# Last stage of an attention and feed-forward kernel: VectorE's gated product placed ahead of Newton's steps, ScalarE's gate and square ahead of the normalisations

## The chip, the cores and the metric

The kernel runs on one core of a Trainium2 chip. The metric is the device time of one execution in microseconds (us). The engines are TensorE (PE in the profile; its weight loads are PEld), VectorE (DVE), ScalarE (ACT), GpSimd (POOL) and SyncE (SP), which here issues all the transfers. Each engine runs its own list of instructions in order and waits on semaphores for the others.

## The reference

A pre-norm transformer layer in fp32: attention, then a gated channel mix that also looks at the token before. The change touches only the second half.

```python
x = x + attention(layernorm(x))               # x: 4 x 2048 x 256, 16 heads of 16
h = layernorm(x)
h_prev = h shifted by one token (zero at the start of a sequence)
hr = mu_r * h + (1 - mu_r) * h_prev
hk = mu_k * h + (1 - mu_k) * h_prev
r = sigmoid(hr @ W_r.T)
k = square(relu(hk @ W_k.T))
x = x + r * (k @ W_v.T)
```

## The kernel before

The 8192 tokens are cut into 16 blocks of 512. A first stage makes q, k and v, a second does attention for 64 steps, and the last stage (`stage_mix`) does the output projection, the second layer norm and the channel mix, block by block, software-pipelined in pairs of blocks (b, b+1 with b even). Nothing schedules at build time: the order on each engine is the order in which its Python function issues calls, and `Steps` objects are semaphores that count named steps ("gated" of block 3, say). The names of the steps:

- `proj(b)` (TensorE, L447) multiplies the attention heads by the output weights; `residual(b)` (VectorE, L367) adds x to it, which gives x1, and takes statistics (L371).
- `means(pair)` (VectorE, L378 to L386) combines the statistics of a pair of blocks and makes a seed for the reciprocal root. `newton(pair)` (L394, L396, L398 three times, then L402) refines it: ten operations on 128x8 elements, all of whose inputs lie in SBUF, and each waits for the one before. The last one gives the offset. Pair p is blocks 2p and 2p+1.
- `normalise(b)` (ScalarE, L1670, four operations) waits for the offset; `turned(b)` (TensorE, L457) transposes its four results one by one; `keep_turned(b)` (ScalarE, L1682 and L1688) copies them out of PSUM and scales them by mu.
- `shift(b)` (VectorE, L412 or L410, then L417 twice for mk and twice for mr) adds the shares of the token before.
- `key(b)` (TensorE, L1783) needs the mk part of `shift(b)`, `receptance(b)` (L1795, weights r) the mr part. `keep_gate(b)` (ScalarE, L1706) is the sigmoid of the receptance, `square(b)` (ScalarE, L1696 relu and L1700 square) works on the key, `value(b)` (TensorE, L1795, weights v) multiplies the square.
- `gated(b)` (VectorE, L1735) multiplies value(b) from PSUM by the gate. `finish(b)` (GpSimd, L1646) adds x1, and SyncE stores the block.
- GpSimd also does `heads(b)` (L321, two operations: attention sums times inverse denominators, for `proj(b)`) and `add_to_x(b)` (L330: x plus bias, for `residual(b)`), in this order for an even b: finish(b), heads(b+6), finish(b+1), add_to_x(b+6), heads(b+7), add_to_x(b+7). Both wait for transfers of their inputs.

TensorE's order in a pair is key(b), receptance(b), value(b), receptance(b+1), key(b+1), turned(b+2), proj(b+4), value(b+1), turned(b+3), proj(b+5). key(b) writes the two PSUM banks that value(b-1) was in, so it waits for gated(b-1):

```python
        elif blk < LAST - 1:
            vy.wait(te, blk - 1, "gated")
```

In the last pairs there is no projection left: after key(13) come turned(14), turned(15), value(13), key(14). value(b) waits for square(b). In this section and below a "pair b" is the stretch from key(b) to key(b+2) on TensorE.

Of the kernel before, what the change touches and what calls it, by code (L numbers as in the profile page):

```python
# [22 lines left out]
B, N, C, H = 4, 2048, 256, 16  # L23
# [4 lines left out]
BLOCKS = B * N // TB  # L28
# [173 lines left out]
class MixInputs:  # L202
# [156 lines left out]
    def residual(self, dve, blk, banks):  # L359

        s = blk % 2
        self.gx.wait(dve, blk, "xb")
        if blk >= SUMS:
            self.gy.wait(dve, blk - SUMS, "y")
        for b in range(2):
            self.pf.wait(dve, blk, ("proj0", "proj")[b])
            self.dx.done(dve.tensor_tensor(self.rows_of(self.x1[blk % SUMS][:, 2 * b:2 * b + 2, :]), banks[b],  # L367
                                      self.rows_of(self.x_sb[s][:, 2 * b:2 * b + 2, :]), ALU.add))
        for t in range(TT):
            self.dx.wait(dve, blk, f"x1{t // 2}")  # L370
            self.ln.done(dve.bn_stats(self.stats[:, s * TT + t, :], self.x1[blk % SUMS][:, t, :]))  # L371
# [1188 lines left out]
def stage_mix(ctx, nc, psum, inputs, out):  # L1560
# [22 lines left out]
    EARLY, LAST = inputs.EARLY, BLOCKS - 1  # L1583

    def turned_at(blk):

        return OUT if blk == LAST else TURNED

    def key_at(blk):
        return {LAST - 1: TURNED, LAST: OUT}.get(blk, KEY)  # L1590

    def rec_at(blk):
        return {0: TURNED, LAST: KEY}.get(blk, REC)

    def squares_of(blk):

        if blk < LAST:
            return inputs.kr, inputs.ka
        return [x1[n % SUMS].rearrange("p t c -> p (t c)").rearrange("p (k t) -> p k t", k=KH)
                for n in (LAST - 5, LAST - 4)]  # L1600

    def after(eng, sem, value):
        if value > 0:
            eng.wait_ge(sem, value)

    def rows_of(t):
        return t.rearrange("p t c -> p (t c)")

    def banks(n):
        return psum[:, n:n + 2, :].rearrange("p a c -> p (a c)")  # L1610
# [52 lines left out]
    def scalar(ac):  # L1663
        def normalise(blk):
            ln.wait(ac, blk // 2, "offset")
            if blk >= 2:
                pt.wait(ac, blk - 2, "turned1")
            for t in range(TT):
                at_t = blk % 2 * TT + t
                an.done(ac.activation(xn[blk % 2][:, t, :], x1[blk % SUMS][:, t, :], ACT.Identity,  # L1670
                                      bias=work[:, 5, at_t:at_t + 1], scale=work[:, 2, at_t:at_t + 1]))

        def keep_turned(blk):

            s = blk % 2
            for k in range(KH):
                pt.wait(ac, blk, f"turned{k}")
                if blk >= 1:
                    vb.wait(ac, blk - 1, "prev")
                if blk >= 2:  # L1680
                    vb.wait(ac, blk - 2, f"mr{KH - 1}")
                at.done(ac.copy(xT[s][:, k, 1:TB + 1], psum[:, turned_at(blk) + k, :]))  # L1682
            for n in ("mk", "mr"):
                if blk >= 2:
                    (pk if n == "mk" else pr).wait(ac, blk - 2, n[1])
                for k in range(KH):
                    at.wait(ac, blk, f"xT{k}")
                    at.done(ac.activation(mixed[n][s][:, k, :], xT[s][:, k, 1:TB + 1], ACT.Copy,  # L1688
                                          scale=col[n][:, k:k + 1]))

        def square(blk):
            kr, ka = squares_of(blk)
            pk.wait(ac, blk, "k")
            if blk == LAST:
                gy.wait(ac, LAST - 4, "y")
            ab.done(ac.activation(kr[:, :, :], psum[:, key_at(blk):key_at(blk) + 2, :], ACT.Relu))  # L1696
            ab.wait(ac, blk, "relu")
            if 1 <= blk < LAST:
                pv.wait(ac, blk - 1, "v")
            ab.done(ac.activation(ka[:, :, :], kr[:, :, :], ACT.Square))  # L1700

        def keep_gate(blk):
            pr.wait(ac, blk, "r")
            if blk >= 2:
                vy.wait(ac, blk - 2, "gated")
            ag.done(ac.activation(rows_of(gate[blk % 2]), banks(rec_at(blk)), ACT.Sigmoid))  # L1706

        for steps in (ab, ag):
            steps.start(ac)
        for blk in range(0, BLOCKS, 2):  # L1710
            more = blk + 2 < BLOCKS
            square(blk)
            keep_gate(blk)
            if more:
                normalise(blk + 2)
                keep_gate(blk + 1)
                normalise(blk + 3)
                square(blk + 1)
            else:
                square(blk + 1)  # L1720
                keep_gate(blk + 1)
            if more:
                for n in range(2):
                    keep_turned(blk + 2 + n)

    def vector(dve):
        def residual(blk):
            inputs.residual(dve, blk, [psum[:, OUT + b, :] for b in range(2)])

        def gated(blk):  # L1730
            s = blk % 2
            pv.wait(dve, blk, "v")
            ag.wait(dve, blk, "gate")
            after(dve, s_out[s], DMA * (blk // 2))
            vy.done(dve.tensor_tensor(rows_of(y[s]), banks(key_at(blk)), rows_of(gate[s]), ALU.mult))  # L1735

        def last_half(half):

            s, at_t = LAST % 2, slice(2 * half, 2 * half + 2)
            pv.wait(dve, LAST, ("half", "v")[half])  # L1740
            if half == 0:
                ag.wait(dve, LAST, "gate")
                dve.wait_ge(s_out[s], DMA * (LAST // 2))
            vy.done(dve.tensor_tensor(rows_of(y[s][:, at_t, :]), psum[:, key_at(LAST) + half, :],
                                      rows_of(gate[s][:, at_t, :]), ALU.mult))
            vy.wait(dve, LAST + half, "gated")
            dve.tensor_tensor(y[s][:, at_t, :], y[s][:, at_t, :], x1[LAST % SUMS][:, at_t, :], ALU.add
                              ).then_inc(s_last, 1)

        vy.start(dve)  # L1750
        for blk in range(0, BLOCKS, 2):
            gated(blk)
            if blk == 0:
                for n in range(inputs.SLICES):
                    inputs.invert(dve, B - 1, n)
            if blk + 4 < BLOCKS:
                residual(blk + 4)
            if blk + 2 < BLOCKS:
                inputs.shift(dve, blk + 2)
            if blk + 1 < LAST:  # L1760
                gated(blk + 1)
            else:
                for half in range(2):
                    last_half(half)
            if blk + 4 < BLOCKS:
                residual(blk + 5)
            if blk + 2 < BLOCKS:
                inputs.shift(dve, blk + 3)
            if blk + 4 < BLOCKS:
                inputs.means(dve, blk // 2 + 2)  # L1770
                inputs.newton(dve, blk // 2 + 2)

    def key(te, blk):
        vb.wait(te, blk, f"mk{KH - 1}")
        if blk == 0:
            dx.wait(te, 2 * EARLY - 1, "x11")
        elif blk < LAST - 1:
            vy.wait(te, blk - 1, "gated")
        else:
            at.wait(te, blk, "xT1")  # L1780
        for h in range(KH):
            for k in range(KH):
                mm = te.matmul(psum[:, key_at(blk) + h, :], w_sb["k"][:, k, h * P:(h + 1) * P],  # L1783
                               mixed["mk"][blk % 2][:, k, :], start=(k == 0), stop=(k == KH - 1))
        pk.done(mm)
# [6 lines left out]
    def tensor(te):  # L1792
# [41 lines left out]
        for blk in range(0, BLOCKS, 2):  # L1834
# [16 lines left out]
            if more:  # L1851
                turned(blk + 3)
                proj(blk + 5)

    return sync, gpsimd, scalar, vector, tensor, first_key


def build(nc, a):
# [7 lines left out]
    with ExitStack() as ctx:  # L1866
# [4 lines left out]
        first = stage_attend(ctx, nc, psum, a["x"], a["wqT"], a["wkT"], a["wvT"], a["bq"], a["bk"], q_d, k_d, kd_d, v_d,  # L1871
                             sums_d, attend_inputs, mix_inputs)
        last = stage_mix(ctx, nc, psum, mix_inputs, a["out"])
        block = ctx.enter_context(nc.Block())

# [47 lines left out]
```

## Time and profile before

| | us |
|---|---|
| median of three runs | 2774.69 (2774.01 to 2775.11) |
| the profiled execution | 2775.01 |
| its span in the trace | 2773.2 |
| last stage in that span, from key(0) on | 2541.7 to the end, 231.5 |
| TensorE busy in 2600 to 2650 | 48.42 of 50.00 |
| VectorE, ScalarE, GpSimd busy there | 37.72, 26.09, 27.14 |
| granted TensorE clock in the last stage | 1.00 (2.4 GHz) |

The span is what the trace covers; the device time of the same execution is 1.8 us longer. Times in the trace count from the start of the span. A row of the timeline is a run of equal instructions, so its length is from the start of the first to the end of the last, and "idle before" is how long its engine had nothing to do, with what ended that.

### The profile page before, as it was taken

How to read it: one execution, taken by the hardware profiler on the slowest of the kernel's cores; microseconds unless marked ns; L12 is line 12 of the kernel's file. 1: busy time of each engine (PE TensorE's matmuls, PEld its weight loads, DVE VectorE, ACT ScalarE, POOL GpSimd, SP SyncE). 2: the span in 40 equal slices, each digit the busy share in tenths (PEclk: the TensorE clock that was granted, in tenths of full speed). 3: DMA queues.
4: the chain of work that ended last, by engine and by line, in shares of the span. 5: the costliest groups of instructions: out<-in, count | busy, mean ns of one | idle time of the engine just before them, and what ended most of it. 6: DMA issues, size and time to landing. Idle time of an engine off the chain costs nothing.

```text
span 2773.2 us, 60078 instructions
## 1 busy us (share of the span) xinstructions
PE 2737.5 (99%) x23666; PEld 927.5 (33%) x23666; DVE 2496.9 (90%) x4853; ACT 2489.6 (90%) x2863; POOL 372.7 (13%) x751
## 2 busy tenths in 40 slices
PE   9999999999999999999999999999999999999999
PEld 6552222222222222222222222222222222224776
DVE  5658999999999999999999999999999999975774
ACT  7768999999999999999999999999999999997555
POOL 6761000000000000000000000000000000103551
PEclk9999999999999999999999999999999999999999
DMA  6642010000000000000010101010101100212531
GB/s 196 208 150 66 12 30 14 22 20 20 22 22 22 22 22 22 23 20 25 11 30 9 33 11 33 12 33 11 33 12 38 29 19 22 59 40 83 163 127 46
DMA packets 135290, 124.36 MB, mean 45 GB/s; under 512 B 49888, under 2 KB 117344, under 8 KB 135008
## 3 DMA queue, kind: packets, MB, share of 16 engines
q1 hardware_dynamic: 135008, 120.52, 14.1%
q8 instruction: 187, 3.06, 0.5%
q14 instruction: 95, 0.78, 0.1%
HBM read 72.75 MB, written 47.19 MB: 43 GB/s over the span
## 4 chain that ended last, share of the span: by engine, by line
PE 81%; SPq 10%; ACT 4%; DVE 2%; DMA 2%; issue 2%; POOL 0%; ACTq 0%; POOLq 0%
PE psum L1364 33%; PE psum L1267 17%; PE psum L1323 15%; PE psum L1392 4%; SPq L153 3%; PE psum L1795 3%; SPq L158 2%; PE psum L1282 2%; PE psum L1405 2%; SPq L126 2%; PE psum L447 2%; SPq L127 2%; DMA a_qs<-q_parts 2%; PE psum L1783 2%; ACT m_gate L963 1%
## 5 line engine op out<-in xcount | busy, mean ns | idle before, releaser
L1045 DVE TENSOR_REDUCE a_mx<-psum 128x1 f32<-128x512 f32 x3096 | 1946.5, 683 | 108.9 <-PE psum L1323 88.4
L1267 PE MATMUL psum<-a_qs,a_ks 50*128 50x512 f16 x4096 | 791.7, 383 | 10.2 <-ACT p_x L963 0.5
L963 ACT ACTIVATE m_gate<-psum 128x1024 f32<-128x1024 f32 x684 | 674.7, 1034 | 37.1 <-PE psum L1267 34.4
L963 ACT ACTIVATE m_y<-psum 128x1024 f32<-128x1024 f32 x682 | 672.7, 1034 | 37.7 <-PE psum L1267 34.8
L1323 PE MATMUL psum<-a_ks,a_qs 48*128 48x512 f16 x3596 | 695.0, 383 | 11.5 <-DVE a_mx L1045 2.4
L963 ACT ACTIVATE p_x<-psum 128x1024 f32<-128x1024 f32 x682 | 672.7, 1034 | 37.3 <-PE psum L1267 34.6
L1364 PE MATMUL psum<-m_gate,a_vst 128*32 128x256 f32 (+1 forms) x4568 | 413.1, 433 | 0.8
L1364 PE MATMUL psum<-p_x,a_vst 128*32 128x256 f32 (+1 forms) x4568 | 412.0, 432 | 0.8
L1364 PE MATMUL psum<-m_y,a_vst 128*32 128x256 f32 (+1 forms) x4552 | 411.8, 433 | 0.8
L1267 PEld LDWEIGHTS psum<-a_qs,a_ks 50*128 50x128 f16 x4096 | 198.8, 93 | 604.7 <-issue 139.6
L1040 DVE CUSTOM_DVE_ANT_0 a_copied<-psum,a_copied 128x512 f32<-128x512 f32 x500 | 323.4, 684 | 22.0 <-PE psum L1323 22.0
L1323 PEld LDWEIGHTS psum<-a_ks,a_qs 48*128 48x128 f16 x3596 | 174.9, 93 | 462.6 <-DVE a_mx L1045 367.2
L972 ACT ACTIVATE a_copied<-psum 128x1024 f32<-128x1024 f32 x250 | 260.5, 1042 | 0.1
L830 POOL MEMSET a_mx<- 128x8 f32 x64 | 7.2, 112 | 1380.5 <-DVE a_m L1024 1345.2
L823 POOL COPY a_vst<-a_vin 128x64 f32<-128x64 f32 x256 | 59.7, 236 | 751.5 <-PE psum L1364 751.5
L1364 PEld LDWEIGHTS psum<-m_gate,a_vst 128*32 128x32 f32 x4568 | 90.4, 107 | 189.8 <-issue 174.7
L1364 PEld LDWEIGHTS psum<-p_x,a_vst 128*32 128x32 f32 x4568 | 90.6, 107 | 189.3 <-issue 173.8
L1364 PEld LDWEIGHTS psum<-m_y,a_vst 128*32 128x32 f32 x4552 | 90.1, 107 | 189.1 <-issue 173.8
L1282 PE MATMUL psum<-a_kd,a_qs 48*128 48x512 f16 x500 | 97.2, 381 | 0.0
L845 POOL TENSOR_TENSOR m_split<-m_whole,m_split 128x512 f16<-128x512 f32 x64 | 73.5, 1159 | 58.4 <-ACT m_split L951 42.1
L949 ACT ACTIVATE m_whole<-psum,p_sb,p_gain 128x512 f32<-128x512 f32 x64 | 49.7, 777 | 34.8 <-PE psum L1392 34.8
L367 DVE TENSOR_TENSOR m_whole<-psum,m_x 128x512 f32<-128x512 f32 x24 | 16.4, 688 | 59.5 <-PE psum L447 59.5
(149 smaller groups left out, 1644.0 us busy)
## 6 DMA issues: line engine op xcount, KB each, us to landing
m_x<-x SPq DMA_DIRECT2D x24, 512.0 KB, 5.7
a_qs<-q_parts SPq DMA_DIRECT2D x384, 32.0 KB, 2.1
sums<-a_o SPq DMA_DIRECT2D x256, 34.0 KB
q_parts<-m_split SPq DMA_DIRECT2D x16, 512.0 KB, 3.2
v_rows<-m_v SPq DMA_DIRECT2D x16, 512.0 KB, 2.8
k_parts<-m_split SPq DMA_DIRECT2D x16, 512.0 KB, 3.9
a_ks<-k_parts SPq DMA_DIRECT2D x64, 128.0 KB
a_vin<-v_rows SPq DMA_DIRECT2D x64, 128.0 KB, 5.7
```

What stands on the lines that cost most here:

```text
L153: sp.dma_start(self.qs[row:row + D, it % QRING, :].rearrange("p (u t) -> p u t", u=GP), src[a, par]).then_inc(self.s_q, DMA)
L845: least.done(pool.tensor_tensor(parts[s][:, j, 1, :], full[s][:, j, :], parts[s][:, j, 0, :], ALU.subtract))
L963: ac.activation(p_sb[n % WEIGHTS][:, 2 * pair:2 * pair + 2, :], psum[:, at:at + 2, :], ACT.Exp, scale=SCALE).then_inc(s_exp, 1)
L972: ac.activation(copied[:, :, :], psum[:, at:at + 2, :], ACT.Relu).then_inc(s_exp, 1)
L1040: dve.tensor_tensor_reduce(out=copied[:, par, :], in0=psum[:, bank(at), :], in1=copied[:, par, :], scale=1.0, scalar=LEAST, op0=ALU.add, o ...
L1045: dve.tensor_reduce(peak, psum[:, bank(at), :], AX.X, ALU.max).then_inc(s_mx, 1)
L1267: mm = te.matmul(psum[:, pair_of_banks(u) + par, :], ks[row:row + MR, (it // QB) % 2, pair, c * P:(c + 1) * P], qs[row:row + MR, it % QRIN ...
L1282: mm = te.matmul(psum[:, pair_of_banks(u) + par, :], qs[row:row + SR, pit % QRING, at:at + P], kd[row:row + SR, (pit // QB) % 2, pair, :], ...
L1323: te.matmul(psum[:, bank(slot(n, par)), :], qs[row:row + SR, pit % QRING, at:at + P], keys, start=True, stop=True).then_inc(s_sp, 1)
L1364: mm = te.matmul(psum[32 * g:32 * g + 32, O, at:at + width], v_st[:, c, g, :], p_sb[n % WEIGHTS][:, g, at:at + width], start=(c == 0), sto ...
L1392: mm = te.matmul(psum[:, j % 2, :], w_sb[n][:, k, h * P:(h + 1) * P], xnT[blk % 2][:, k, :], start=(k == 0), stop=(k == KH - 1))
L1795: mm = te.matmul(psum[:, bank + t // 2, (t % 2) * C:(t % 2 + 1) * C], lhsT[:, k, t * P:(t + 1) * P], w[:, k, :], start=(k == 0), stop=(k = ...
```

## The change

Three moves, all in `stage_mix`. No instruction is added or removed, except that the listing below groups neighbours.

1. VectorE: gated(b), for even b from 2 to 14, now stands in front of newton, directly after means (for b = 14, where there is no newton, its place is as before). Before, it came after newton, as the first call of the next round.
2. VectorE, first pair only: gated(1) now stands between residual(4) and shift(2), before after shift(2).
3. ScalarE: before, the order was normalise(b+2), keep_gate(b+1), normalise(b+3), square(b+1), keep_turned(b+2), keep_turned(b+3); now it is keep_gate(b+1), normalise(b+2), square(b+1), normalise(b+3), and then the same.

```diff
@@ scalar
             square(blk)
             keep_gate(blk)
             if more:
+                keep_gate(blk + 1)
                 normalise(blk + 2)
-                keep_gate(blk + 1)
+                square(blk + 1)
                 normalise(blk + 3)
-                square(blk + 1)
+                for n in range(2):
+                    keep_turned(blk + 2 + n)
@@ vector
-        for blk in range(0, BLOCKS, 2):
-            gated(blk)
-            if blk == 0:
-                for n in range(inputs.SLICES):
-                    inputs.invert(dve, B - 1, n)
-            if blk + 4 < BLOCKS:
-                residual(blk + 4)
-            if blk + 2 < BLOCKS:
+        gated(0)
+        for n in range(inputs.SLICES):
+            inputs.invert(dve, B - 1, n)
+        residual(4)
+        gated(1)
+        inputs.shift(dve, 2)
+        for blk in range(0, LAST - 1, 2):
+            if blk:
+                if blk + 4 < BLOCKS:
+                    residual(blk + 4)
                 inputs.shift(dve, blk + 2)
-            if blk + 1 < LAST:
                 gated(blk + 1)
...
             if blk + 4 < BLOCKS:
                 residual(blk + 5)
-            if blk + 2 < BLOCKS:
-                inputs.shift(dve, blk + 3)
+            inputs.shift(dve, blk + 3)
             if blk + 4 < BLOCKS:
                 inputs.means(dve, blk // 2 + 2)
+            gated(blk + 2)
+            if blk + 4 < BLOCKS:
                 inputs.newton(dve, blk // 2 + 2)
+        for half in range(2):
+            last_half(half)
```

The orders of TensorE, GpSimd and SyncE are the same in both. On VectorE, in the first pair, with the gated product as L1735 before and L1734 after:

```order
-L1735 TENSOR_TENSOR m_y<-psum,m_gate 128x1024
+L1734 TENSOR_TENSOR m_y<-psum,m_gate 128x1024
 L291 RECIPROCAL m_inv<-m_den 128x32 x8
 L367 TENSOR_TENSOR m_x<-psum,m_x 128x512 x2
 L371 BN_STATS m_stats<-m_x 128x6 x4
+L1734 TENSOR_TENSOR m_y<-psum,m_gate 128x1024
 L412 COPY m_xT<-m_xT 128x2
 L417 SCALAR_TENSOR_TENSOR m_split<-m_xT,m_restmk,m_split 128x512 x2
 L417 SCALAR_TENSOR_TENSOR m_split<-m_xT,m_restmr,m_split 128x512 x2
-L1735 TENSOR_TENSOR m_y<-psum,m_gate 128x1024
```

gated(1) moved past the five instructions of shift(2). On VectorE, in a later pair, between the seed (L386) and Newton's first step (L394):

```order
 L382 TENSOR_SCALAR m_work<-m_work 128x8
 L386 TENSOR_SCALAR m_work<-m_work 128x8
+L1734 TENSOR_TENSOR m_y<-psum,m_gate 128x1024
 L394 TENSOR_TENSOR m_work<-m_work 128x8
 L396 SCALAR_TENSOR_TENSOR m_work<-m_work 128x8
```

The even block's product now stands there; it is gone from its place behind the last of the ten steps (L402). On ScalarE, in the same pair, after the even block's square (L1696, L1700):

```order
-L1706 ACTIVATE m_gate<-psum 128x1024
-L1670 ACTIVATE m_xn<-m_x,m_work 128x256 x4
-L1706 ACTIVATE m_gate<-psum 128x1024
+L1706 ACTIVATE m_gate<-psum 128x1024 x2
 L1670 ACTIVATE m_xn<-m_x,m_work 128x256 x4
 L1696 ACTIVATE m_v<-psum 128x1024
 L1700 ACTIVATE m_v<-m_v 128x1024
+L1670 ACTIVATE m_xn<-m_x,m_work 128x256 x4
 L1682 COPY m_xT<-psum 128x512 x2
```

The two gates stand together, then come the first normalisation, the square, and the second normalisation.

## Rows read from the trace of the kernel before

**Rows 1.** Timeline of PE, pair 4: start us, us, engine line op out<-in xcount [idle]

```profile
2602.34 3.60 PE L1783 MATMUL psum<-m_split,m_wk 128*128 128x512 f32 x8
...
2612.74 3.72 PE L1795 MATMUL psum<-m_wr,m_split 128*128 128x256 f32 x16
2617.18 3.67 PE L1783 MATMUL psum<-m_split,m_wk 128*128 128x512 f32 x8 [0.71 <-DVE m_y L1735]
2620.68 1.04 PE L457 MATMUL psum<-m_ident,m_xn 128*128 128x128 f32 x8
...
2632.80 3.60 PE L1783 MATMUL psum<-m_split,m_wk 128*128 128x512 f32 x8
```

**Rows 2.** Timeline of DVE, same pair: means, Newton's steps, gated(4).

```profile
2605.87 3.40 DVE L417 SCALAR_TENSOR_TENSOR m_split<-m_xT,m_restmk,m_split 128x512 f32<-128x512 f32 x2
...
2612.61 0.63 DVE L378 BATCH_NORM_AGGREGATE m_mv<-m_stats 128x2 f32<-128x6 f32 x8
...
2613.89 0.17 DVE L394 TENSOR_TENSOR m_work<-m_work 128x8 f32<-128x8 f32 x1
...
2615.70 0.17 DVE L402 SCALAR_TENSOR_TENSOR m_work<-m_mv,m_work 128x8 f32<-128x8 f32 x1
2615.80 1.22 DVE L1735 TENSOR_TENSOR m_y<-psum,m_gate 128x1024 f32<-128x1024 f32 x1
```

**Rows 3.** Timeline of ACT, same pair: normalise(6).

```profile
2615.90 2.07 ACT L1670 ACTIVATE m_xn<-m_whole,m_work 128x256 f32<-128x256 f32 x4 [5.44 <-DVE m_work L402]
```

**Rows 4.** Timeline of POOL, same pair: finish(4).

```profile
2617.11 2.36 POOL L1646 TENSOR_TENSOR m_y<-m_y,m_x 128x1024 f32<-128x1024 f32 x1 [4.97 <-DVE m_y L1735]
```

**Rows 5.** Timeline of all engines: a Newton step beside a GpSimd addition.

```profile
2543.57 2.35 POOL L330 TENSOR_TENSOR m_x<-m_x,m_bo 128x1024 f32<-128x1024 f32 x1 [1.97 <-DMA m_x<-x]
2543.61 2.33 DVE L394 TENSOR_TENSOR m_work<-m_work 128x8 f32<-128x8 f32 x1
```

**Rows 6.** Timeline of PE, first pairs: value(1) and key(2).

```profile
2564.55 3.62 PE L1795 MATMUL psum<-m_wv,m_v 128*128 128x256 f32 x16
...
2572.93 3.67 PE L1783 MATMUL psum<-m_split,m_wk 128*128 128x512 f32 x8 [0.43 <-DVE m_y L1735]
```

**Rows 7.** Timeline of DVE, first pairs: shift(2), gated(1), residual(5), shift(3).

```profile
2567.95 2.38 DVE L417 SCALAR_TENSOR_TENSOR m_split<-m_xT,m_restmk,m_split 128x512 f32<-128x512 f32 x2
...
2571.57 1.21 DVE L1735 TENSOR_TENSOR m_y<-psum,m_gate 128x1024 f32<-128x1024 f32 x1
2572.71 1.27 DVE L367 TENSOR_TENSOR m_x<-psum,m_x 128x512 f32<-128x512 f32 x2
...
2575.22 0.14 DVE L412 COPY m_xT<-m_xT 128x2 f32<-128x2 f32 x1
```

**Rows 8.** Timeline of POOL, first pairs: heads(6), add_to_x(6), add_to_x(7).

```profile
2566.62 2.49 POOL L321 TENSOR_TENSOR m_hT<-m_num,m_rden 128x512 f32<-128x512 f32 x2 [9.43 <-DMA m_rden<-inverse_denominators]
...
2577.54 2.81 POOL L330 TENSOR_TENSOR m_x<-m_x,m_bo 128x1024 f32<-128x1024 f32 x1 [2.31 <-DMA m_x<-x]
...
2587.76 2.36 POOL L330 TENSOR_TENSOR m_x<-m_x,m_bo 128x1024 f32<-128x1024 f32 x1 [4.96 <-DMA m_x<-x]
```

**Rows 9.** Timeline of PE, pair 12: value(12), receptance(13), value(13).

```profile
2731.55 3.62 PE L1795 MATMUL psum<-m_wv,m_v 128*128 128x256 f32 x16
2735.00 3.62 PE L1795 MATMUL psum<-m_wr,m_split 128*128 128x256 f32 x16
...
2744.26 3.72 PE L1795 MATMUL psum<-m_wv,m_v 128*128 128x256 f32 x16 [0.46 <-ACT m_v L1700]
```

**Rows 10.** Timeline of DVE, same pair: gated(12).

```profile
2735.20 1.23 DVE L1735 TENSOR_TENSOR m_y<-psum,m_gate 128x1024 f32<-128x1024 f32 x1 [2.32 <-PE psum L1795]
```

**Rows 11.** Timeline of ACT, same pair: normalise(15), square(13), keep_turned(14).

```profile
2739.57 2.06 ACT L1670 ACTIVATE m_xn<-m_whole,m_work 128x256 f32<-128x256 f32 x4
2742.09 1.03 ACT L1696 ACTIVATE m_v<-psum 128x1024 f32<-128x1024 f32 x1 [0.45 <-PE psum L1783]
...
2744.11 1.06 ACT L1682 COPY m_xT<-psum 128x512 f32<-128x512 f32 x2
```

More of the change, by code:

```diff
@@ L1721, in scalar @@
                 keep_gate(blk + 1)
-            if more:
-                for n in range(2):
-                    keep_turned(blk + 2 + n)
     def vector(dve):
@@ L1750, in vector @@
         vy.start(dve)
-        for blk in range(0, BLOCKS, 2):
-            gated(blk)
-            if blk == 0:
-                for n in range(inputs.SLICES):
-                    inputs.invert(dve, B - 1, n)
-            if blk + 4 < BLOCKS:
-                residual(blk + 4)
-            if blk + 2 < BLOCKS:
+        gated(0)
[8 more added lines that the diff above has]
+                    residual(blk + 4)
                 inputs.shift(dve, blk + 2)
-            if blk + 1 < LAST:
                 gated(blk + 1)
-            else:
-                for half in range(2):
-                    last_half(half)
             if blk + 4 < BLOCKS:
                 residual(blk + 5)
-            if blk + 2 < BLOCKS:
-                inputs.shift(dve, blk + 3)
+            inputs.shift(dve, blk + 3)
             if blk + 4 < BLOCKS:
                 inputs.means(dve, blk // 2 + 2)
+            gated(blk + 2)
+            if blk + 4 < BLOCKS:
                 inputs.newton(dve, blk // 2 + 2)
+        for half in range(2):
+            last_half(half)
     def key(te, blk):
```

## The prediction

> **What bounds the kernel now.** I read the timeline of TensorE first, then those of the engines that it waits for. In the last stage TensorE works nearly without a gap, so a gain can only come out of its gaps. The one that repeats: receptance(5) starts at 2612.74, key(5) at 2617.18 [rows 1]. A stage of sixteen such matmuls takes 3.45 from start to start (2731.55 to 2735.00) [rows 9], 3.5 behind a wait (2617.18 to 2620.68) [rows 1]; key(5) could have started at 2616.25 and is 0.93 late, with VectorE's gated product named as releaser. The reason stands in the order of VectorE [rows 2]: means begin at 2612.61, Newton's steps at 2613.89, the product only at 2615.80. Four pairs (4, 6, 8, 10) look like this. key(2) has a gap of 0.43 for gated(1) [rows 6], and value(13) one of 0.46 for square(13) [rows 9]. The prize is thus about 4 x 1.0 + 0.5 + 0.5, 5 us of 2775: 0.18% at the very best. (A measurement of this kernel can tell about 0.2%, 5.5 us, from no change.)
>
> **What comes in place of the gap, pairs 4 to 10.** gated(4) moves ahead by Newton's ten steps. Means to product takes 1.18 (the product follows its predecessor by 0.10, L394 stands 1.28 behind L378) [rows 2], so it starts at G = 2613.79 and ends at 2615.01. key(5) goes at 2616.25: the gap is gone, with 1.2 us to spare, and turned(6) could start at 3.44 more, 2619.69 (no wait ahead of it).
> But GpSimd's finish(4) starts 1.31 after the product does (2615.80 to 2617.11) and runs 2.36 [rows 2, 4]. Before, VectorE had nothing to do then. Now Newton's steps begin at G + 1.14 (2571.57 to 2572.71 for what follows a product) [rows 7], and the second at G + 1.34, 0.03 after finish(4). What a small VectorE step does beside a GpSimd addition can be seen once [rows 5]: L394, 0.17 us long elsewhere [rows 2], took 2.33, from 0.04 after the addition began until it ended. So the second step waits until G + 1.31 + 2.36 = G + 3.67; eight more follow at 0.20 each (1.81 for nine from 2613.89 to 2615.70) [rows 2], the last starts at G + 5.12 and normalise(6) 0.20 later [rows 2, 3], at G + 5.3 = 2619.1. Its 2.07 us end at 2621.2; the last two transposes need some 0.3 behind that (0.05 from releaser to start, two of eight transposes in 0.88, the rate of a restart). proj(8) starts at 2621.5. Before, it started at 2620.68 + 0.88 = 2621.56 [rows 1]. The 0.93 is given back almost exactly one stage later: **-0.1 per pair, -0.35 for four** (between -0.6, if the step wins the port from GpSimd now and then, and 0). Everything behind proj keeps its distance to it: square(5) follows normalise(6) and is done 1.5 before value(5), and shift(6) waits for proj(8) anyway. Covered by this: the later normalise(7) and keep_turned(6), some 2 us nearer to their users, 1 us or more left.
> The rows show this for L394 and not for a small SCALAR_TENSOR_TENSOR (seven of the ten steps). The Trainium skill ("SBUF — State Buffer", section "Who interferes with whom") says that a VectorE instruction with two SBUF inputs contends with a GpSimd one that reads SBUF, and that the later one blocks until the first is done. All ten steps have two such inputs; the rule speaks against this change, and L394 at 2.33 agrees. Without such a rule the sum would be the lock-free rival below.
>
> **First pair and pair 2.** gated(1) can start 3.65 after value(1) does (2731.55 to 2735.20 for block 12) [rows 9, 10]: 2564.55 + 3.65 = 2568.20 [rows 6]. finish(1), which was at 2572.86, now goes at 2569.50 to 2571.86, and shift(2) begins at 2569.34, right under it. A blocked mk pair ends 1.22 after GpSimd lets go (heads(6) until 2569.11, pair until 2570.33) [rows 7, 8]: 2573.08. key(2) starts at 2573.14, against 2572.93 before [rows 6]: +0.2 where -0.5 was meant.
> shift(3) suffers more. From the end of mk to the end of mr is 1.24 (2570.33 to 2571.57), and residual(5) with its statistics takes 2.51 (2572.71 to 2575.22) [rows 7], so shift(3) begins at 2573.08 + 1.24 + 2.51 = 2576.83, 1.6 later than before. add_to_x(6) comes at 2577.54, when its input lands [rows 8], heads(7) behind it; before, shift(3) was nearly through. Now GpSimd gets the port after the first mk step, at 2577.76, holds it 2.21 (its end was 2580.35, 2.21 after shift(3) let it in), and the other three steps go one by one between its operations: 0.55 after 2579.97, then 1.70 each, as beside heads(9) (3.40 for two) [rows 2]: 2583.9. receptance(3) could start at 2573.14 + 3.5 + 2 x 3.45 = 2583.55; it starts at 2583.97, **+0.4**, and key(3) at 2587.5, turned(4) at 2590.9.
> Then Newton again: means at 2583.85, G = 2585.05, the steps from 2586.2, the ninth at 2587.80 and the tenth at 2588.0. add_to_x(7) starts at 2587.76, when its input lands [rows 8]; nothing in the change moves that transfer. It blocks the ninth step until 2590.1, and finish(2), which is next on GpSimd, blocks the tenth until 2592.45. normalise(4) runs from 2592.5 to 2594.55, and proj(6) starts at 2594.85, where the free order of TensorE gives 2591.75. Before, key(2) at 2572.93 and 3.5 + 4 x 3.45 + 0.88 behind it gave 2591.1. So **pair 2 ends 3.7 later than before**. This hangs on 0.04 us for the second block and on 0.25 for the first: if the ninth step slips in ahead, normalise(4) goes at 2590.2 and the pair loses 1.4; if both do, 0.65.
>
> **Pair 12, the last.** Here value(12) sets the product: G = 2735.20 [rows 10]. The same Newton delay puts normalise(14) at G + 5.3 = 2740.5 to 2742.6, so square(13), which was at 2742.09 [rows 11], goes at 2742.5; and normalise(15), which stood ahead of it (2739.57), now stands behind it. square takes 2.02 (2742.09 to 2744.11) [rows 11], normalise 2.07: 2746.6. turned(15) is ahead of value(13) on TensorE, and needs it: value(13) starts at 2746.87 against 2744.26 [rows 9], **+2.6**. Until the end TensorE then waits for nothing else: keep_turned(14), shift(14), gated(13) are 2.4 later, less than that. In the other pairs this move costs nothing, since proj and value stand between.
>
> **Sum:** +3.7 - 0.35 + 2.6 = +6.0, a profiled execution of 2781.0, and against the median of 2774.69 (0.32 below the profiled one) **2780.7**.
>
> **Rivals.**
> (a) *One step slips in*, or both, in pair 2: +1.4 or +0.65 in place of +3.7, so 2778.4 or 2777.6: no difference to be measured. For it: the margin is a few hundredths. Against: I counted no waits but those in rows, and any more makes it two.
> (b) *Not slower, lock-free*: Newton's steps run at 0.20 beside GpSimd. Then key(2) wins 0.6 and pairs 4 to 10 win 1.0 each; pair 12 still loses 2.2 (normalise(15) behind square(13): 2744.1 + 2.07 + 0.3 = 2746.45). Sum -2.4, 2772.3. Against it: [rows 5]. It decides from the point where Newton's second step ends before G + 2.
> (c) *Faster by 0.2%* would need lock-free and no loss in pair 12: 2769.5. ScalarE's order forbids it.
> (d) *Every pair pays*: add_to_x(b+5) ended 1.65 before G in pair 4. Should its input land that much later, it blocks Newton's steps too, up to 2.36 per pair: 2783 and more. Against it: that transfer keeps its distance to proj.
>
> **How the numbers follow.** Forecast with two blocks 0.45, (a) 0.39 (0.27 and 0.12), (b) 0.05, (c) 0.03, (d) and other losses 0.08. The range reaches from (a) at 2777.6 less 0.5 for its terms to 2782.0, the forecast with 0 for -0.35 and a later transfer: 2777.0 to 2782.0. The bound of 0.2% is 2780.24, half a microsecond under the forecast, so a quarter of its chance counts as no change: slower 0.41 (0.34 + 0.07), same 0.55, faster 0.04.
>
> **What would show it.** Right: key(5), key(7), key(9), key(11) without a wait, but turned(6) and so on waiting for normalise; one step of Newton of some 2.3 us directly behind each even product; two of them in pair 2; receptance(3) late; value(13) near +2.6 over its place. Wrong: Newton's steps all at 0.17, or proj(8) more than 0.3 nearer to key(4) than 19.2 us (2602.34 to 2621.56) [rows 1], or a ScalarE wait in pair 12 that is not for VectorE's offset.

## The result, and the profile after

| | us |
|---|---|
| before, median of 16 | 2774.15 |
| after, median of 16 | 2778.64 (2777.42 to 2785.48) |
| ratio | 1.0018, 95% interval 1.0011 to 1.0025 |
| the profiled execution of after | 2783.50, its span 2781.7 |

The change makes the kernel 4.5 us slower, inside the range of 2777.0 to 2782.0 and 2.1 below the 2780.7 that was forecast. (0.5 of these 2.1 come from the base: the forecast stood on a median of three, 2774.69, and that of sixteen is 2774.15. As a change it was +4.5 for a forecast of +6.0.) Of the 16 executions nine lie between 2777.4 and 2778.8, four between 2779.3 and 2780.1, and three (one of them the profiled one) above 2782: they are not all alike, and the reading of one trace alone would mislead. So two more executions of the same program were profiled (after_look1 and after_look2, below).

The measure used from here on is the length of a pair, from key(b) to key(b+2) on TensorE. It leaves out the stages ahead of key(0), which is at 2541.3 to 2544.5 in the fourteen profiles of this case, whatever the kernel.

| pair | before | forecast | after | look1 | look2 |
|---|---|---|---|---|---|
| 0 | 31.23 | 31.44 | 31.43 | 31.45 | 31.44 |
| 2 | 29.41 | 32.9 | **34.03** | **34.63** | 29.45 |
| 4 | 30.46 | 30.37 | 29.78 | 29.79 | 29.90 |
| 6 | 30.70 | 30.6 | 30.73 | 30.71 | 30.69 |
| 8 | 30.45 | 30.36 | 30.40 | 30.38 | 30.43 |
| 10 | 30.71 | 30.6 | 30.67 | 30.69 | 30.70 |
| 12 | 23.16 | 25.8 | 27.26 | 25.69 | 27.12 |
| key(14) to last value | 17.22 | 17.22 | 17.22 | 17.22 | 17.23 |

Timeline of TensorE in the profile of after, pair 6, the answer to [rows 1] (start us, us, engine line operation, idle before and its releaser). key(7) is the second row:

```profile
2647.99 3.72 PE L1795 MATMUL psum<-m_wr,m_split 128*128 128x256 f32 x16 [0.22 <-DVE m_split L417]
2651.54 3.60 PE L1783 MATMUL psum<-m_split,m_wk 128*128 128x512 f32 x8
2655.09 1.82 PE L457 MATMUL psum<-m_ident,m_xn 128*128 128x128 f32 x8
2656.75 3.62 PE L447 MATMUL psum<-m_wo,m_hT 128*128 128x256 f32 x16
```

key(7) has no wait any more (the 0.22 ahead of receptance(7) is the wait for shift(7), 0.15 before). The eight transposes of turned(8), which took 1.04 in [rows 1], take 1.82, since they wait one by one for ScalarE. VectorE in the same stretch, the answer to [rows 2]:

```profile
2649.04 1.22 DVE L1734 TENSOR_TENSOR m_y<-psum,m_gate 128x1024 f32<-128x1024 f32 x1
2650.18 0.16 DVE L394 TENSOR_TENSOR m_work<-m_work 128x8 f32<-128x8 f32 x1
2650.37 2.34 DVE L396 SCALAR_TENSOR_TENSOR m_work<-m_work 128x8 f32<-128x8 f32 x1
```

and GpSimd and ScalarE, the answers to [rows 4] and [rows 3]:

```profile
2650.34 2.35 POOL L1646 TENSOR_TENSOR m_y<-m_y,m_whole 128x1024 f32<-128x1024 f32 x1 [3.62 <-DVE m_y L1734]
```
```profile
2654.35 2.08 ACT L1670 ACTIVATE m_xn<-m_whole,m_work 128x256 f32<-128x256 f32 x4 [1.58 <-DVE m_work L402]
```

The product starts at G = 2649.04, finish(6) at G + 1.30, the second of Newton's steps at G + 1.33, and it waits to the end of that addition: an instruction on 128x8 elements takes 2.34. normalise(8) starts at G + 5.31, as the forecast had it to 0.01.

Pair 2 of the same profile: VectorE's steps of Newton that are not 0.15 to 0.17 long, and GpSimd beside them, the answer to [rows 8]:

```profile
2587.45 2.26 DVE L398 SCALAR_TENSOR_TENSOR m_work<-m_work 128x8 f32<-128x8 f32 x1
2589.75 2.26 DVE L394 TENSOR_TENSOR m_work<-m_work 128x8 f32<-128x8 f32 x1
```
```profile
2587.35 2.34 POOL L330 TENSOR_TENSOR m_x<-m_x,m_bo 128x1024 f32<-128x1024 f32 x1 [3.68 <-DMA m_x<-x]
2589.65 2.34 POOL L1646 TENSOR_TENSOR m_y<-m_y,m_whole 128x1024 f32<-128x1024 f32 x1
```

Two steps are held, the sixth behind add_to_x(7), the seventh behind finish(2). Pair 2 and pair 12 on TensorE, the latter to be read beside [rows 9]:

```profile
2593.39 2.08 PE L457 MATMUL psum<-m_ident,m_xn 128*128 128x128 f32 x8 [1.97 <-ACT m_xn L1670]
2595.26 4.60 PE L447 MATMUL psum<-m_wo,m_hT 128*128 128x256 f32 x16
...
2749.62 2.08 PE L457 MATMUL psum<-m_ident,m_xn 128*128 128x128 f32 x8 [2.14 <-ACT m_xn L1670]
2751.49 4.99 PE L1795 MATMUL psum<-m_wv,m_v 128*128 128x256 f32 x16
2756.32 3.60 PE L1783 MATMUL psum<-m_split,m_wk 128*128 128x512 f32 x8
```

Both places have something that the forecast did not: behind a wait of about 2 us, sixteen matmuls of 128x256 take 4.60 and 4.99 where they take 3.62 elsewhere. The granted clock (the figure of 1.00, 0.60 and so on, behind the busy times of PE, PEld, DVE, ACT and POOL) shows why:

```profile
2588.00:2593.30 5.30, 3.42 (x8) 1.15 (x7) 4.47 (x5) 1.68 (x3) 3.99 (x2) 1.00 0.44 159
2593.30:2596.00 2.70, 2.61 (x10) 1.92 (x11) 0.00 (x0) 2.67 (x5) 0.00 (x0) 0.60 0.47 155
2596.00:2600.00 4.00, 4.00 (x17) 3.40 (x17) 0.80 (x2) 4.00 (x8) 0.00 (x0) 0.85 0.00 0
2600.00:2604.00 4.00, 4.00 (x24) 3.57 (x23) 3.95 (x9) 2.10 (x4) 2.51 (x2) 1.00 0.46 134
...
2749.50:2752.00 2.50, 2.27 (x10) 1.51 (x11) 0.06 (x1) 2.50 (x6) 0.00 (x0) 0.77 0.02 7
2752.00:2756.00 4.00, 4.00 (x15) 3.34 (x14) 2.84 (x5) 4.00 (x8) 0.00 (x0) 0.72 0.01 2
```

TensorE was at 2.4 GHz (1.00) until it had idled for 1.97 us, then fell to 1.2 GHz for part of the next two windows (0.60 and 0.85), and was back at 2600. From the start of proj(6) to that of value(3) are 4.44 us in place of 3.45: the clock cost 1.0 there, and 1.3 in pair 12 (value(13) to key(14) is 4.83 against 3.56 before; with the slower transposes of turned(15) it is 1.6, the difference between pair 12 here and in look1).

The wait in pair 12 comes from ScalarE, to be read beside [rows 11]. normalise(15) stood ahead of square(13) there; now it is the row of 2748.89, behind it, and turned(15) waits for it:

```profile
2744.92 2.08 ACT L1670 ACTIVATE m_xn<-m_whole,m_work 128x256 f32<-128x256 f32 x4 [0.84 <-DVE m_work L402]
2746.90 1.00 ACT L1696 ACTIVATE m_v<-psum 128x1024 f32<-128x1024 f32 x1
...
2748.89 2.06 ACT L1670 ACTIVATE m_xn<-m_whole,m_work 128x256 f32<-128x256 f32 x4
```

### The profile page after: what moved, and what is told of

The parts are those of the page before. It is cut to its first block, busy times and chain, and to the rows that moved or that the text cites. A ratio compares the mean times of both kernels' runs of the same rounds, so it can differ in the third digit from the quotient of the medians.

```text
span 2781.7 us, 60078 instructions
## 1 busy us (share of the span) xinstructions
PE 2744.8 (99%) x23666; PEld 928.7 (33%) x23666; DVE 2511.6 (90%) x4853; ACT 2489.4 (89%) x2863; POOL 374.8 (13%) x751
## 4 chain that ended last, share of the span: by engine, by line
PE 80%; SPq 9%; ACT 4%; DVE 3%; issue 2%; DMA 2%; POOL 0%; ACTq 0%; POOLq 0%
PE psum L1364 33%; PE psum L1267 17%; PE psum L1323 15%; PE psum L1392 4%; SPq L153 3%; PE psum L1282 2%; SPq L158 2%; PE psum L1405 2%; PE psum L1795 2%; PE psum L447 2%; SPq L126 2%; SPq L127 2%; DMA a_qs<-q_parts 2%; ACT m_gate L963 1%; ACT p_x L963 1%
## 5 line engine op out<-in xcount | busy, mean ns | idle before, releaser
L963 ACT ACTIVATE m_gate<-psum 128x1024 f32<-128x1024 f32 x684 | 674.3, 1033 | 37.2 <-PE psum L1267 34.4
L1706 ACT ACTIVATE m_gate<-psum 128x1024 f32<-128x1024 f32 x16 | 16.4, 1024 | 56.6 <-PE psum L1795 56.6
```

The costliest lines, as they stand in the source:

```text
L963: ac.activation(p_sb[n % WEIGHTS][:, 2 * pair:2 * pair + 2, :], psum[:, at:at + 2, :], ACT.Exp, scale=SCALE).then_inc(s_exp, 1)
```

## The experiments

The theory after this reading had four parts. (1) In pairs 4 to 12 finish(b), which the product itself releases, holds one of Newton's steps, and that costs what key(b+1) gains. (2) In pair 2 it depends on when the input of add_to_x(7) lands. (3) In pair 12 there is no stage left that covers the later normalise(15), so its delay shows. (4) The long waits of (2) and (3) also cost TensorE its clock. All runs of a comparison shared their chip with runs of the kernel before, whose medians were 2774.2 to 2774.5.

### The addition off the port

finish_waits adds one wait on GpSimd:

```diff
         def finish(blk):
             vy.wait(pool, blk, "gated")
+            if blk % 2 == 0 and 2 <= blk <= 12:
+                ln.wait(pool, blk // 2 + 1, "offset")
```

> The changed kernel, and GpSimd's finish(b) of an even b from 2 to 12 also waits for the offset that Newton's steps make, so no such addition runs beside them. Lock theory: Newton's ten steps take 1.8 us in pairs 4 to 12, normalise(b+2) follows gate(b+1) at once, turned(b+2) does not wait; pairs 4 to 10 become 1.0 us shorter than before each (-4.0), pair 12 keeps +2.2 and perhaps its clock (+1.3) because normalise(15) still stands behind square(13), pair 2 loses 0.5 to 1.5 (add_to_x(7) can still block one step, finish(2) no longer): -1.5 to +1 us against the kernel before, 4 us less than the changed one. Lock-free rival (the steps are slow or late for another reason): steps as in the changed kernel, and the same time as it, +4.5.

Measured: 2774.98 against 2774.45, ratio 1.0002 (0.9994 to 1.0011). Its pairs: 31.57, 29.44, **29.34, 29.76, 29.49, 29.77**, 26.96. Pairs 4 to 10 are 1.12, 0.94, 0.96 and 0.94 shorter than before, 3.96 in sum. Timeline of VectorE and, in the second fence, of GpSimd in its pair 4, around gated(4) (here L1736):

```profile
2614.25 1.23 DVE L1736 TENSOR_TENSOR m_y<-psum,m_gate 128x1024 f32<-128x1024 f32 x1
2615.39 0.16 DVE L394 TENSOR_TENSOR m_work<-m_work 128x8 f32<-128x8 f32 x1
2615.58 0.17 DVE L396 SCALAR_TENSOR_TENSOR m_work<-m_work 128x8 f32<-128x8 f32 x1
...
2617.18 0.17 DVE L402 SCALAR_TENSOR_TENSOR m_work<-m_mv,m_work 128x8 f32<-128x8 f32 x1
```
```profile
2617.49 2.36 POOL L1648 TENSOR_TENSOR m_y<-m_y,m_x 128x1024 f32<-128x1024 f32 x1 [3.62 <-DVE m_work L402]
```

The same ten steps, at the same place in the order, take 1.8 us once the addition comes after them. That settles part (1) against its rival: the step is not slow by itself. The theory's +2.2 and 1.3 for pair 12 are there as well (value(13) +2.43 and the stage behind it +1.37, 3.80 in sum). Pair 2 had no blocked step in this profile, where the theory had a loss of 0.5 to 1.5; the first pair lost 0.34.

### One part of the change at a time

scalar_only has ScalarE's new order, vector_only VectorE's; the other engine is as before.

```diff
# scalar_only, against the changed kernel
+        inputs.shift(dve, 2)
         gated(1)
-        inputs.shift(dve, 2)
...
+            if blk + 4 < BLOCKS:
+                inputs.newton(dve, blk // 2 + 2)
             gated(blk + 2)
-            if blk + 4 < BLOCKS:
-                inputs.newton(dve, blk // 2 + 2)
```
```diff
# vector_only, against the changed kernel
+                normalise(blk + 2)
                 keep_gate(blk + 1)
-                normalise(blk + 2)
-                square(blk + 1)
                 normalise(blk + 3)
+                square(blk + 1)
```

> ScalarE's new order alone, VectorE as before. Theory: the gaps before key(5), key(7), key(9), key(11) stay as before (0.93 each), normalise(b+2) is later but still ahead of turned(b+2); pair 12 loses 2.2 us because normalise(15) stands behind square(13), plus up to 1.3 where the clock falls: +2.2 to +3.6 us against the kernel before. Rival (ScalarE's order costs nothing by itself, only together with the blocked steps): within 0.7 us of the kernel before.

Measured: 2778.15 against 2774.37, ratio 1.0013 (1.0003 to 1.0023). Pairs 2 to 10 as before (29.42, 30.31, 30.68, 30.46, 30.73), key(5) with its old wait of 0.73; pair 12 is 26.98, 3.8 longer. ScalarE's move alone loses in pair 12 what was expected, clock included. Its medians of +3.8 are 0.2 above the upper end that I had set.

> VectorE's new order alone, ScalarE as before. Theory: a blocked step makes normalise(b+2) 3 us later, and gate(b+1), normalise(b+3) and square(b+1) stand behind it, so square(b+1) ends some 1.2 us after value(b+1) could start: pairs 4 to 10 last 1.0 us longer than before each, pair 12 loses 3.5 and its clock 1.3, the first pairs 0.2 to 5: +9 to +14 us. So ScalarE's move pays for VectorE's. Rival (the two moves are independent, ScalarE has slack): pairs 4 to 10 as in the changed kernel, pair 12 +1 or less: within +2 us of the kernel before.

Measured: 2782.11 against 2774.37, ratio 1.0028 (1.0018 to 1.0039), +7.7: slower than with both moves, so the rival falls, but below the +9 that the theory gave. Its pairs are 31.73, 29.45, 31.03, 30.75, 30.74, 30.76, 28.03. The mechanism is there, in pair 4 value(5) waits for square(5):

```profile
2627.20 3.72 PE L1795 MATMUL psum<-m_wv,m_v 128*128 128x256 f32 x16 [0.98 <-ACT m_v L1700]
```

but the wait stands against the gap at key(5) that the product's move had taken away, so a pair lasts 0.05 to 0.57 more than before, and not 1.0; I had counted the wait at 1.2 and the gain at 0.1, since I took the gain as already spent on turned(6). Together with ScalarE's order the wait is gone: square(b+1) no longer stands behind two normalisations.

### The first pair

```diff
# first_undone, against the changed kernel
         residual(4)
+        inputs.shift(dve, 2)
         gated(1)
-        inputs.shift(dve, 2)
```

> The changed kernel, but gated(1) stands behind shift(2) again; the rest of the change stays. Theory (GpSimd's finish(1) blocks shift(2), that pushes shift(3) under add_to_x(6) and heads(7), and that pushes Newton's steps for blocks 4 and 5 under add_to_x(7) and finish(2)): key(2) is back at its old place, shift(3) runs free in 2.8 us, all ten steps of Newton in pair 2 take 0.17, turned(4) does not wait for normalise(4). Against the kernel before: pairs 4 to 10 -0.4 to -0.7, pair 12 +2.8 and its clock +1.3, together +3.5 us, and no executions beyond +6. Rival (the losses of pair 2 come from the product ahead of Newton's steps alone, not from the first pair): pair 2 still has one or two blocked steps, +4.5 to +8 as in the changed kernel.

Measured: 2777.86 against 2774.45, ratio 1.0013 (1.0003 to 1.0022): +3.4 for the +3.5 expected. (One of the eleven executions, at 8894 us, was disturbed; the median without it is 2777.55, +3.1.) The others lie at 2775.9 to 2779.6, none above +6. Its pair 2 is 29.41, as before. Pair 12 is 25.68: the same late normalise(15), but value(13) to key(14) took 3.46, so here the clock had not fallen behind the same wait:

```profile
2743.58 1.82 PE L457 MATMUL psum<-m_ident,m_xn 128*128 128x128 f32 x8 [2.14 <-ACT m_xn L1670]
```

The profile bears out the mechanism of the first pair and of pair 2, but not the sum: it is of the shortest execution (2775.89), its pairs 4 to 10 are 1.4 shorter than before and not 0.4 to 0.7, and without the fall of the clock it has only +0.9 from key(0) on. That the median came out as expected does not show that each term did.

### The same program again, and the input of add_to_x(7)

> The changed kernel again, for the profile of another execution. Theory (the loss in pair 2 hangs on when the inputs of add_to_x(7) land: 45.3 us after key(0) in the first profile, two blocked steps): where they land 46.3 us or more after key(0), Newton's steps in pair 2 all take 0.17 and pair 2 lasts 29.5 us; at 45.9 or less two steps are blocked and it lasts 33 or more; pairs 4 to 10 and 12 look as in the first profile, value(13) 22.2 to 22.4 behind key(12). Rival (the two blocks come from the order alone): pair 2 lasts 33 us or more in every profile.

> The same kernel once more, with the same expectations: either a pair 2 without blocked steps or one with two, by the landing of that input, while each of pairs 4 to 12 has exactly one blocked step.

The first was 2781.82, the second 2778.80. In look1 add_to_x(7) started at 2586.95, 45.65 after its key(0), and two steps of Newton were held (2.36 and 2.27); pair 2 lasted 34.63. In look2 it started at 2588.68, 46.80 after key(0), the last step was done at 2587.67, and pair 2 lasted 29.45. VectorE in look2:

```profile
2577.21 1.42 DVE L417 SCALAR_TENSOR_TENSOR m_split<-m_xT,m_restmk,m_split 128x512 f32<-128x512 f32 x2
2578.54 4.52 DVE L417 SCALAR_TENSOR_TENSOR m_split<-m_xT,m_restmr,m_split 128x512 f32<-128x512 f32 x2
2582.99 0.63 DVE L378 BATCH_NORM_AGGREGATE m_mv<-m_stats 128x2 f32<-128x6 f32 x8
```

The input of add_to_x(6) was later too (2578.28, 36.40 after key(0), against 35.71 in after), so the mk pair of shift(3) ran free and shift(3) as a whole ended 1.0 us earlier against key(0) than in after (2583.06 and 2584.21). Both things work the same way: later inputs, fewer held steps. The expectation's two limits (46.3 and 45.9) held, with nothing in between seen. Pair 12 of look1 did not look as in the first profile: value(13) came at 22.23 as expected, but without the fall of the clock.

Why the input lands at different times can be read from SyncE. It waits for its store of the inverse denominators to land, and only then issues the rest of the stage's transfers, one behind the other:

| | before | after | look1 | look2 |
|---|---|---|---|---|
| SyncE's wait for that store, us | 8.6 | 9.3 | 8.7 | 10.8 |
| load for add_to_x(7) issued, after key(0) | 34.84 | 34.36 | 34.43 | 35.44 |
| add_to_x(7) starts, after key(0) | 46.06 | 45.33 | 45.65 | 46.80 |
| from issue to start | 11.22 | 10.97 | 11.22 | 11.36 |

Of the 1.47 us between after and look2, 1.08 are in the issue and 0.39 in the load itself. A late store moves the inputs of add_to_x(6) and add_to_x(7) together.

To turn this into a cause, input_waits takes the coincidence away:

```diff
                 inputs.heads(pool, blk + 7)
+                if blk == 0:
+                    ln.wait(pool, 2, "offset")
                 inputs.add_to_x(pool, blk + 7)
```

> The changed kernel, and GpSimd's add_to_x(7), with finish(2) behind it, waits until Newton's steps for blocks 4 and 5 are done; nothing else is moved. Theory (the executions above 2779.5 us of the changed kernel are those in which the input of add_to_x(7) lands while Newton's steps run): pair 2 lasts 29.4 to 30 us in the profile, no blocked step in it, and in the rounds the tail above 2780 is gone: median +4.0 us against the kernel before, highest below 2780.5. Rival (the slow executions come from the clock in pair 12 or from the stages ahead): the spread stays, with some in ten above 2780.5.

Measured: 2778.73 against 2774.19, ratio 1.0013 (1.0004 to 1.0022). Eleven executions lie between 2777.48 and 2779.74. The median is that of the changed kernel, and the tail is absent: of 16 executions of the changed one 5 were above 2780, here none of 11 (which would come about by chance once in 18 times), and none of the ten undisturbed ones of first_undone. Pair 2 is 29.93, with no step held. So add_to_x(7) beside Newton's steps makes most of the tail, and not the median. It does not make all of it: one of the ten executions of scalar_only, where Newton's steps stand as before, took 2783.73, and no profile shows why.

### The last pair

last_undone has the old order in pair 12 only, on both engines:

```diff
-            gated(blk + 2)
+            if blk != 10:
+                gated(blk + 2)
             if blk + 4 < BLOCKS:
                 inputs.newton(dve, blk // 2 + 2)
+            if blk == 10:
+                gated(blk + 2)
...
-            if more:
+            if blk == 12:
+                normalise(blk + 2)
+                keep_gate(blk + 1)
+                normalise(blk + 3)
+                square(blk + 1)
+            elif more:
                 keep_gate(blk + 1)
```

> The changed kernel, but pair 12 has the old order on both engines: Newton's steps ahead of gated(12), and normalise(14), gate(13), normalise(15), square(13). Theory (value(13) waits for turned(15), that for normalise(15), which stands behind square(13) and behind steps of Newton blocked by finish(12); and the wait lets TensorE's clock fall): value(13) starts 19.6 us behind key(12) instead of 22.4, takes 3.56 instead of 4.83 until key(14), so 4.1 us less than the changed kernel in every execution: about +0.4 us against the kernel before in its quick executions, up to +4.5 where two steps are blocked in pair 2. Rival (the order of the last pair is hidden, the loss is all in pair 2): within 1 us of the changed kernel, +3.5 or more.

Measured: 2774.83 against 2774.45, ratio 1.0004 (0.9996 to 1.0013), with executions from 2773.9 to 2779.1: +0.4 and a tail to +4.7, as expected. Pair 12 is 23.15, and value(13) 19.59 behind key(12). The median loss of the changed kernel sits in this one pair. Its profile also shows what the first pair can do: heads(6), whose input landed 2.4 later against key(0) than in after (2568.40 for 2566.32, with key(0) 0.35 earlier), and finish(1) directly behind it both held shift(2), and key(2) waited 1.81; pair 0 took 32.60.

### The clock

gap_filled puts sixteen matmuls, overwritten afterwards, ahead of turned(15):

```diff
                 dx.wait(te, LAST, "x11")
+                for _ in range(16):
+                    te.matmul(psum[:, turned_at(LAST), 0:P], ident[:, :], ident[:, :], start=True, stop=True)
```

> The changed kernel with sixteen 128x128 matmuls, whose result is overwritten, ahead of turned(15), in the 2.1 us in which TensorE waits for normalise(15). Clock theory (the granted clock falls in or after that wait, and turned(15) and value(13) then run slower): the clock stays at 1.00 in pair 12, value(13) to key(14) takes 3.5 instead of 4.8, and turned(15) does not last longer than 1.9; up to 1.4 us less than the changed kernel, +2 to +4.5 against the one before. Rival (the slow stage has another reason, such as the weights of value(13) or the port): value(13) still takes 4.8 in its profile, and the time is that of the changed kernel or above.

Measured: 2779.74 against 2774.48, ratio 1.0019 (1.0010 to 1.0028). That is +5.3, above the expected +2 to +4.5. Timeline of TensorE in its pair 12, and the granted clock there:

```profile
2742.85 3.74 PE L1812 MATMUL psum<-m_ident 128*128 128x128 f32 x32
2746.42 1.04 PE L457 MATMUL psum<-m_ident,m_xn 128*128 128x128 f32 x8
2747.30 3.62 PE L1795 MATMUL psum<-m_wv,m_v 128*128 128x256 f32 x16
```
```profile
2744.00:2748.00 4.00, 4.00 (x36) 3.92 (x35) 0.17 (x1) 4.00 (x9) 0.00 (x0) 1.00 0.00 0
2748.00:2752.00 4.00, 4.00 (x17) 2.99 (x16) 3.79 (x5) 4.00 (x9) 0.00 (x0) 1.00 0.01 2
```

The clock stayed up and value(13) took its 3.45. But the filler ran 3.57 us (it is counted as 32), longer than the wait it was to fill, and made value(13) 0.3 later (22.71 behind key(12), 22.43 in after). The time is not below that of the changed kernel, as the rival had it. That the filler keeps the clock is consistent with the clock theory and no proof of it, since three other profiles (first_undone, look1, input_waits) kept it without one; as a remedy it bought nothing that could be measured.

In the seven profiles in which turned(15) waits 1.9 to 2.1 us, the stage behind it took 4.68 to 5.14 in four (after, look2, scalar_only, finish_waits) and 3.46 or 3.45 in three, with no difference in the wait that I can name; in vector_only, with waits of 1.05 and 1.56 close together, it took 5.16. What decides it stays open.

### Putting it together

both_ends_finish_waits has the wait of finish_waits for pairs 2 to 10, and the old order in the first pair and in pair 12. first_guarded is the same with gated(1) ahead of shift(2), and finish(1) held:

```diff
         def finish(blk):
             vy.wait(pool, blk, "gated")
+            if blk == 1:
+                vb.wait(pool, 2, f"mr{KH - 1}")
```

> The wait of the kernel labelled finish_waits in pairs 2 to 10, with the first pair and pair 12 in the old order. If the three places are independent as the theory has them: pairs 0 and 2 as before, pairs 4 to 10 -1.0 us each, pair 12 as before: -4.0 us against the kernel before, about 2770.1, no execution much above that. Rival (what is won in front of key(5) is always given back by a later wait of the same pair): within 1 us of the kernel before.

> The kernel labelled both_ends_finish_waits, but with gated(1) ahead of shift(2) and GpSimd's finish(1) held until shift(2) is through. If finish(1) under shift(2) is what made the first pair lose: key(2) starts 3.45 behind proj(5) without a wait where heads(6) is through in time, 0.3 to 0.6 us less than both_ends_finish_waits, so -3.5 us against the kernel before. Rival (holding finish(1) pushes add_to_x(6) and heads(7) further onto shift(3) and means): the same or up to 1 us more than both_ends_finish_waits.

> The same kernel as both_ends_finish_waits, on the same chip as the two above, for comparison with first_guarded: -3 to -4 us against the kernel before, pairs 4 to 10 within 0.1 us of 29.34, 29.75, 29.50, 29.76.

| | this | before, same chip | ratio |
|---|---|---|---|
| both_ends_finish_waits | 2771.42 | 2774.45 | 0.9988 (0.9979 to 0.9997) |
| both_ends_again | 2770.79 | 2774.48 | 0.9988 (0.9979 to 0.9997) |
| first_guarded | 2770.18 | 2774.48 | 0.9987 (0.9978 to 0.9996) |

These beat both kernels, by 3.0 to 4.3 us against the one before (for the -4.0, -3.5 and -3 to -4 expected) and by 7 to 8.5 against the changed one, so the rival of the first is out. Pairs 4 to 10 of both_ends_again are 29.34, 29.77, 29.55, 29.76. TensorE's wait list has no row for key(b) on the gated product any more, and GpSimd waits, harmlessly, for Newton's last step (who waited for whom in first_guarded, total, times, longest):

```profile
POOL m_y L1650 <- DVE m_work L402: 19.7, 4, 5.6
```

Between the last two kernels of the table the difference (0.6) is inside what such runs scatter. Their profiles differ by 0.12 us from key(0) to the last value stage, so the first pair's move is worth nothing that can be told: in all three, pair 0 lasted 30.63 to 30.68. In the two of both_ends heads(6) still held shift(2) (its mk pair took 2.38, as before), but it started 24.3 after key(0) and not 24.9 as before, so gated(1) was through when TensorE came to key(2). In first_guarded key(2) follows proj(5) by 3.45, without a wait, as expected.

## Why the prediction was right or wrong, point by point

- **Gap at key(5) and its like closed:** right; key(5), key(7), key(9) and key(11) have no wait.
- **Given back at turned(b+2) through one held step of Newton:** right, and to the hundredth where nothing else moved: G + 5.31 in pair 6; pairs 6, 8 and 10 changed by +0.03, -0.05 and -0.04 for the -0.1 of the sum. finish_waits shows the cause by taking it away.
- **Pair 4:** better than forecast, -0.68. The input of add_to_x(9) landed later in all three profiles of after, and the mr pair of shift(5) ran free (1.40 us against 3.50), so gated(4) started 10.83 behind key(4) for 11.45. I had kept that transfer at its distance from before.
- **First pair:** right; +0.20 for +0.21. key(2) had to wait for shift(2) behind finish(1).
- **Pair 2:** the step that failed as a forecast of the median. The mechanism was right (receptance(3) 0.37 late for 0.4; two steps held, and normalise(4) at 2592.65, with key(0) 0.32 later, for 2592.5), and two of three profiles show it. That normalise(4) agrees so closely is in part luck: the input came 0.7 earlier against key(0) than before (45.33 for 46.06), so the sixth and seventh steps were held and not the ninth and tenth, and the three more steps that were left behind them, 0.6, made up for it. But its term of +3.7 holds only where the input of add_to_x(7) lands early; from the tail I count it in 3 of 16 executions, perhaps in 5, and the typical one pays nothing, so rival (a) with both steps through, which had a chance of 0.12, seems to be the usual case. The text said that it hangs on 0.04 us, and then reasoned that anything uncounted would make it two blocks; what was uncounted was that the input comes at 45.3 to 46.8 after key(0) from one execution to the next, mostly because SyncE issues it later behind a late store. That is larger than every margin in that paragraph. It should have been priced as a distribution.
- **Pair 12:** mechanism right, the term too small. value(13) came 22.23 and 22.43 behind key(12) for a forecast of 22.21, and then 1.1 to 1.3 us were added by the clock in the stage behind it, in two of three profiles. No row of before shows a wait of 2 us on TensorE in this stage (the longest is 0.7), so its price stood nowhere in the sum.
- **Sum:** the two errors have opposite signs, and that the forecast came as near as it did is in part luck: without pair 2's +3.5, and with -0.3 more in pairs 4 to 10 together (mostly pair 4) and +1.3 in pair 12, the sum would be +3.5, and look2 has +3.62 between key(0) and the last stage. The median moved by 4.5. The remaining 0.9 is not assigned; executions of different length are mixed in it. The prediction also took 3.7 us as too little to be told from no change; with sixteen executions of each kernel, 4.5 us was told from it (1.0011 to 1.0025).

## What to carry to other kernels

Moving an instruction ahead on one engine also moves what it releases on the others: ask what that work will run beside. Here the released addition on GpSimd held one of the ten small steps of VectorE that now followed the product for 2.2 us; before, VectorE had nothing to do beside it. One semaphore wait that ordered the addition behind those steps was worth 4 us of 2775 (+0.5 us against the kernel before, for +4.5). And a move that pays in the steady pairs has to be looked at in the last pair on its own, where the stages that cover it are missing.

## What the runs showed of the hardware

- A small SCALAR_TENSOR_TENSOR with two SBUF inputs is held by a GpSimd addition just as TENSOR_TENSOR is: 2.34 us for 0.17. The start of one after the other decides by 0.03 us (GpSimd at G + 1.30, VectorE at G + 1.33), in each of the five pairs 4 to 12 of all three profiles of after. The rule that the prediction cites (the Trainium skill, "SBUF — State Buffer", section "Who interferes with whom") agrees with it.
- BATCH_NORM_AGGREGATE is not held by such an addition: eight of them took 0.63 in pair 4 of look2, while add_to_x(9) ran, and the TENSOR_SCALAR behind them took 1.76.
- TensorE's granted clock can fall from 2.4 to 1.2 GHz behind a wait of 2 us (or two of 1.05 and 1.56), in some executions and not in others of the same program, and the sixteen matmuls behind it then take 4.4 to 5.2 us for 3.45.
- In three executions of one program the same input was used at 45.3 to 46.8 us after key(0), 1.5 us apart, in a case where the median time of the kernel before repeats to 0.3 us. 1.1 of it is the issue of the load, behind a wait of 8.7 to 10.8 us for a store to land; the load itself took 11.0 to 11.4 us from issue to use.
